# Two-layer graph network on one core: which count lets GpSimd issue the next gathers of the score stage

## The reference

```python
def _gatv2(x, edge_index, Wl, Wr, att, gat_bias):
    src, dst = (edge_index[0], edge_index[1])
    xl = (x @ Wl).reshape(-1, HEADS, C)
    xr = (x @ Wr).reshape(-1, HEADS, C)
    h = jax.nn.leaky_relu(xl[src] + xr[dst], NEG_SLOPE)
    e = jnp.einsum('ehc,hc->eh', h, att)
    m = jax.ops.segment_max(e, dst, num_segments=N_NODES)
    ex = jnp.exp(e - m[dst])
    denom = jax.ops.segment_sum(ex, dst, num_segments=N_NODES)
    alpha = ex / (denom[dst] + 1e-16)
    msg = alpha[..., None] * xl[src]
    out = jax.ops.segment_sum(msg, dst, num_segments=N_NODES)
...
h = jnp.maximum(_layernorm(x, axis=-1), 0.0)
x = x + _L0_gnn_ref(h, edge_index, ...)
h = jnp.maximum(_layernorm(x, axis=-1), 0.0)
x = x + _L1_gnn_ref(h, src, dst, L1_gnn_ln_g, L1_gnn_ln_b, L1_gnn_W, L1_gnn_b)
```

## Time and profile before

| | us |
|---|---|
| median of 3 runs | 1217.9 |
| the runs | 1214.75 to 1218.52 |
| span of the profiled execution | 1275.0 |
| VectorE busy | 1030.6 (81%) |
| TensorE busy | 1089.3 (85%) |
| ScalarE busy | 681.0 (53%) |
| GpSimd busy | 436.6 (34%) |
| L587, 352 gathers of both stages | 356.8 busy, 235.7 idle before them |
| L1569, 88 weightings | 107.7 busy, 54.4 idle before them |
| L1573, 88 sums | 107.3 busy, 2.7 idle before them |

### The profile page before, as it was taken

One profiled execution on the slowest core, in us unless ns is written; L12 is line 12 of the kernel. 1 busy time (PEld: TensorE's weight loads), 2 busy tenths in 40 slices (PEclk: granted clock), 3 DMA queues, 4 the chain that ended last, 5 costly groups with the idle time before them and its releaser, 6 DMA issues.

```text
span 1275.0 us, 16061 instructions
## 1 busy us (share of the span) xinstructions
PE 1089.3 (85%) x5027; PEld 793.4 (62%) x5047; DVE 1030.6 (81%) x1478; ACT 681.0 (53%) x1264; POOL 436.6 (34%) x412
## 2 busy tenths in 40 slices
PE   3979879566766666499999999799999999999998
PEld 2578456444544444245555555598888888889896
DVE  8999999778777887899999999876766869583934
ACT  4601300465565654478888888767555674232420
POOL 2072073565555666177766665000002100000000
PEclk9989989888777876599999999799999999999999
DMA  5000001566565658266667666400000211000002
GB/s 187 34 10 15 25 10 34 150 168 173 165 173 160 181 166 193 59 165 194 194 191 195 191 191 153 141 1 18 9 9 25 65 38 46 1 18 25 1 1 82
DMA packets 43436, 122.85 MB, mean 96 GB/s; under 512 B 7838, under 2 KB 8626, under 8 KB 43352
## 3 DMA queue, kind: packets, MB, share of 16 engines
q0 software_dynamic: 29184, 93.81, 27.5%
q1 hardware_dynamic: 14168, 27.98, 6.6%
HBM read 116.13 MB, written 5.59 MB: 95 GB/s over the span
## 4 chain that ended last, share of the span: by engine, by line
PE 46%; ACT 7%; DVE 2%; issue 1%; ACTq 1%; another core or an unknown queue 0%; DVEq 0%
PE bank L891 11%; PE bank L851 8%; PE bank L837 8%; PE bank L784 7%; PE bank L907 7%; PE bank L795 5%; ACT counts L1077 3%; ACT hot L964 2%; ACT arena L962 2%; PE bank L822 1%; ACTq L1073 0%; DVE stat L1269 0%; PE bank L625 0%; DVE w_lo L1637 0%
## 5 line engine op out<-in xcount | busy, mean ns | idle before, releaser
L587 POOL DMA_INDIRECT arena<-left_table,arena x352 | 356.8, 1013 | 235.7 <-issue 85.4
L784 PE MATMUL bank<-arena,hot 128*128 128x512 f32 x352 | 177.5, 620 | 0.9 <-DVE den_parts L1661 0.9
L718 PE MATMUL bank<-xr_hi,hot_t 128*128 x176 | 94.9, 539 | 97.3 <-ACT bank L1050 66.7
L1569 DVE SCALAR_TENSOR_TENSOR arena<-bank,arena 128x1024 f32<-128x1024 f32 x88 | 107.7, 1224 | 54.4 <-PE bank L718 29.9
L891 PE MATMUL bank<-counts_r,ns 128*128 128x512 f32 (+2 forms) x720 | 137.1, 349 | 0.0
L891 PEld LDWEIGHTS bank<-counts_r,ns 128*128 128x128 f32 x720 | 125.6, 188 | 10.4
L1077 ACT ACTIVATE counts<-bank 128x1280 f32 x88 | 108.9, 1238 | 37.6 <-issue 21.1
L795 PE MATMUL bank<-arena 128*128 128x512 bf16 (+1 forms) x508 | 110.0, 349 | 9.2 <-ACT counts L1077 5.6
L1050 ACT ACTIVATE bank<-arena 128x1024 f32<-128x1024 f32 x88 | 90.2, 1025 | 42.8 <-DMA arena<-left_table,arena 29.9
L718 PEld LDWEIGHTS bank<-xr_hi,hot_t 128*128 128x128 f32 x176 | 41.9, 238 | 110.4 <-issue 104.9
L1573 DVE TENSOR_REDUCE arena<-arena 128x16 f32<-128x1024 f32 x88 | 107.3, 1220 | 2.7
(11 more groups left out here) (258 smaller groups left out, 2256.2 us busy)
## 6 DMA issues: line engine op xcount, KB each, us to landing
arena<-left_table,arena POOLq DMA_INDIRECT x352
arena<-in_x_dram SPq DMA_DIRECT2D x18, 256.0 KB, 5.0
arena<-in_L_gnn_W_dram SPq DMA_DIRECT2D x8, 512.0 KB
arena<-in_L_gnn_W_dram SPq DMA_DIRECT2D x2, 1536.0 KB, 11.1
arena<-in_L_gnn_W_dram SPq DMA_DIRECT2D x3, 1024.0 KB, 5.3
left_table<-arena SPq DMA_DIRECT2D x10, 260.0 KB, 2.0
out_dram<-state SPq DMA_DIRECT2D x9, 256.0 KB
arena<-in_L_gnn_Wl_dram SPq DMA_DIRECT2D x1, 1024.0 KB, 9.0
```

The lines of the kernel that those rows point to most:

```text
L587: g.indirect_dma_start(out=gathered[n % DEPTH][:, i, :], out_offset=None, in_=left_table, in_offset=bass.IndirectOffsetOnAxis(ap=src_of[:, ...
L718: ins_ = t.matmul(bank[:, rows_at(n) + i, :], mine, part[:, bass.ds(at, 1), :].rearrange("p b n -> p (b n)"), start=False, stop=(part is x ...
L784: t.matmul(bank[:, psum, :], as_float(hot[c % 4]), w[:, i, :], start=(i == 0), stop=(i == 1))
L1569: v.scalar_tensor_tensor(y, bank[:, at:at + 2, :], 0.0, over(att_relu, 1, 2), ALU.max, ALU.mult).then_inc(*rows_weighted.up())
```

## The change

The gates of the score stage's gathers are counts of VectorE instead of TensorE's. The first gather of pair n waits for `rows_weighted` of pair n-4, the second for `pair_scored` of pair n-4. The first four pairs have no gate. The wait for the free buffer stays, and the gathers of the second stage have no gate, as before.

```diff
-    LEADS = 4, 3
+    LEAD = 4
...
-            def gather(n, rows=None):
+            def gather(n, scoring=False):
 
                 for i in range(2):
                     c = 2 * n + i
-                    if rows and n + 1 - rows[i] > 0:
-                        g.wait_ge(rows_added.sem, n + 1 - rows[i])
+                    if scoring and n >= LEAD:
+                        g.wait_ge((pair_scored if i else rows_weighted).sem, n - LEAD + 1)
                     g.indirect_dma_start(out=gathered[n % DEPTH][:, i, :], out_offset=None, in_=left_table,
...
             for n in range(NG):
                 if n >= DEPTH:
                     g.wait_ge(sources_kept.sem, n - DEPTH + 1)
-                gather(n, LEADS)
+                gather(n, True)
```

## The result

The changed kernel takes 1225.4 us (median of 4 runs, 1224.1 to 1227.1), the kernel before 1217.6 (median of 4, 1214.8 to 1218.5): a ratio of 1.0065 with an interval of 1.0048 to 1.0083. It is slower by 7.8 us, over twice the 0.3% that a measurement can tell from no change.

A forecast was written before the change was run, and what follows sets the result against it. VectorE was taken to bound the score stage at 2.51 us a pair. Adding 0 per pair, 0 for held places, 0 at the start and 1.1 at the end to 1217.9 gave 1219.0 us, range 1211 to 1226.

The forecast's parts named there:

- the lost margin: Slower rival, chance 0.26: gather data arrives too late for the reduced lead; 1229 us, or mildly 1222 to 1226.
- The gates and what stands behind them: GpSimd's queue in the score stage: only the awaited count differs, only gathers stand behind it, only the seed waits for those.
- The new loop: Score stage, VectorE taking pair n-4 to pair n ready: 8.8 us against 10.0 for four pairs; cost 0 per pair.
- GpSimd's start: Term of the loop: GpSimd starts a gather 0.3 us after what it waits for, like its gap between gathers.
- Issue to seed: Term of the loop: from the second gather's issue to ScalarE's seed, 3.45 us, read from pair 19.
- The rival's point: Slower rival's threshold: data over 4.6 us from its gather's issue now reaches VectorE; before the change it took 8.5.
- the rival's strong form: Slower rival at a usual data distance of 5.1 us: 22 loops each 0.5 us longer, 11 us, 1229 in all.
- The end: Last pairs of the score stage, holding padding: cost between 0 and 3.4 us, taken as 1.1.
- The held places: Score stage waits for TensorE's late reports: a second gather goes about 1.0 us earlier, booked as a gain of 0.
- No row decides it: Whether timed runs have TensorE's late reports: margin 1.2 us without, 3.0 with; the loop closes within VectorE's time either way.
- What would show it: Profile signs: L587 waits for L1569 and L1573, idle before L1569 50 to 58 us, stage 282 within 3.
- The rival *faster: Score stage gathers freed from TensorE's late reports remove some seed waits: 6 us gained, 1212 us, chance 0.22.

The follow-up runs named there:

- LEADS = 5, 4: The kernel before, with one pair more of lead on each of its gates by TensorE's count; ratio 0.9965 to the kernel before, without late TensorE reports.
- LEAD = 5: The changed kernel with both VectorE counts taken five pairs back, not four; 1.0070, 1.0076 and 1.0050 to the kernel before, on chips with late TensorE reports.
- LEAD = 3: The changed kernel with both VectorE counts taken three pairs back, not four; ratio 1.0173 to the kernel before, on a chip otherwise showing late TensorE reports.

## Why the prediction held in its range and not in its sum, step by step

The range of 1211 to 1226 held the time, 0.6 us from its end, and the direction came out as summed. The sum did not hold: it gave 1.1 us more than before, within what a measurement can't tell from nothing, and 7.8 were measured. It was the rival *the lost margin*, in its mild form (1222 to 1226), with a chance of 0.26. So the range is right through that rival and not through the mechanism that I held for the likeliest, and that is luck in part.

**The gates and what stands behind them**: as told. No instruction's duration changed, and only gathers wait there.

**The new loop of 8.8 us with 1.2 us of cover** is the step that failed. The direction was right, 4 us of margin went, but two terms of what was left were too small. Pair 24 in the profile of after, with VectorE's weighting of pair 20 at its start and that of pair 24 at its end:

```profile
280.94 1.22 DVE L1569 SCALAR_TENSOR_TENSOR arena<-bank,arena 128x1024 f32<-128x1024 f32 x1
...
282.91 0.94 POOL L587 DMA_INDIRECT arena<-left_table,arena  x1 [0.32 <-issue]
...
284.16 0.95 POOL L587 DMA_INDIRECT arena<-left_table,arena  x1 [0.30 <-issue]
...
287.74 1.03 ACT L1050 ACTIVATE bank<-arena 128x1024 f32<-128x1024 f32 x1 [0.99 <-DMA arena<-left_table,arena]
...
289.85 0.40 PE L718 MATMUL bank<-xr_lo,hot_t 128*128 x1
...
290.99 1.22 DVE L1569 SCALAR_TENSOR_TENSOR arena<-bank,arena 128x1024 f32<-128x1024 f32 x1
```

1.22 (weighting) + 0.75 (until the first gather starts) + 1.25 (until the second does) + 3.58 (until the seed) + 2.51 (until the rows are added, at 290.25) = 9.31 us, and VectorE takes four pairs in 10.05. Two terms were mis-sized:

- *GpSimd's start*, booked at 0.3 us behind the sums. The first gather starts 0.75 us behind the weighting (median over pairs 10 to 79, and the least as well), and the second 1.25 later: 1.22 + 0.75 + 1.25 = 3.22 where I had 2.47 + 0.3 = 2.77. With the same 0.75 behind the sums the second gate would give 2.47 + 0.75 = 3.22 as well, so the two gates ask for the same moment and the second adds nothing to the first. The term is 0.45 us too small.
- *Issue to seed*, booked at 3.45 us from a single pair, which lies near the quickest of all. In the profile of after it is 3.76 at the median of the 38 seeds of pairs 10 to 79 that wait for their data, and 5.04 at the worst. That is not a matter of the quiet chip: read in the same way, the profile of before itself gives 3.80 (20 seeds, 3.35 to 5.16), and the two other held ones 3.78 and 3.77. The term is 0.31 us too small, and the trace at hand would have shown it. The Trainium skill, DMA: Bandwidth & Descriptors, section "Latency and other measured facts", has the access to HBM grow with its load; these profiles don't show it in the calm part of the stage, where 3.80 goes with 166 GB/s and 3.76 with 197 (225 to 450 us of each).

In place of 8.8 the loop is 1.22 + 0.75 + 1.25 + 3.76 + 2.47 + 0.1 = 9.55, and the cover 0.5 us, not 1.2. The rows are ready 0.51 us (median) before VectorE takes them, where I expected 1 to 1.5; with LEADS = 5, 4 it is 3.7. Half a microsecond is eaten by anything. Pair 56 shows how, in the timeline of after:

```profile
369.61 0.95 POOL L587 DMA_INDIRECT arena<-left_table,arena  x1 [2.05 <-issue]
...
373.00 1.03 ACT L1050 ACTIVATE bank<-arena 128x1024 f32<-128x1024 f32 x1 [2.80 <-DMA arena<-left_table,arena]
...
375.66 1.23 DVE L1569 SCALAR_TENSOR_TENSOR arena<-bank,arena 128x1024 f32<-128x1024 f32 x1 [1.01 <-PE bank L718]
```

One gather that starts late for no reason that the profile shows, and VectorE loses 1.0 us that it never makes up. Before pair 83 L1569 waits 7.0 of its 11.7 us for L718. This place is 1.0 of them; from 378 to 400 us, where 2.8 more of them stand, the granted clock of TensorE is 0.73 of full speed, against 1.00 in the stretch of pair 24 (280 to 291 us). What each of the others comes of was not traced.

**The rival's point, data over 4.6 us away.** As the calm loop really runs, it is 3.76 + 0.5, about 4.3 us. My figure for the rival's strong form, a usual 5.1, didn't come; the usual distance stayed under the point, and only the spread went over it (4 of the 38 seeds). That is why it is the mild form.

**The end, booked at 1.1 us between 0 and 3.4.** The waits before the weightings of pairs 83 to 87 are 1.09, 0.73, 0.95, 0.80 and 1.15 us, 4.7 in all. How much of it the change added can't be read off, since the kernel before waits there too: 3.5, 3.4 and 3.8 us in its held profiles. With 83 pairs that hold edges and the first called 0, the padding begins with pair 83, not with 84 as I had it, so five such pairs wait and not four. Pair 87 in the timeline of after, from the weighting of pair 83 on:

```profile
450.67 1.23 DVE L1569 SCALAR_TENSOR_TENSOR arena<-bank,arena 128x1024 f32<-128x1024 f32 x1 [1.09 <-PE bank L718]
...
452.65 0.94 POOL L587 DMA_INDIRECT arena<-left_table,arena  x1 [1.38 <-DVE arena L1569]
...
453.90 0.95 POOL L587 DMA_INDIRECT arena<-left_table,arena  x1 [0.30 <-issue]
...
460.76 1.03 ACT L1050 ACTIVATE bank<-arena 128x1024 f32<-128x1024 f32 x1 [2.47 <-DMA arena<-left_table,arena]
...
463.48 0.63 PE L718 MATMUL bank<-xr_lo,hot_t 128*128 x1
464.21 1.23 DVE L1569 SCALAR_TENSOR_TENSOR arena<-bank,arena 128x1024 f32<-128x1024 f32 x1 [1.15 <-PE bank L718]
```

The loop closes to the hundredth: 1.23 + 0.75 + 1.25 + 6.86 + 3.35 + 0.10 = 13.54 us for four pairs, 3.39 each against 2.51. The prediction had 5.40 us for the data of such pairs; here the four seeds of 84 to 87 start 5.88 to 6.86 us behind their second gather, and with TensorE at the lower of its clocks (a granted clock of 0.50 from 452 to 464 us and 0.63 us a matmul, where pair 24 has 1.00 and 0.40) seed to rows takes 3.35, not 2.47. Against LEADS = 5, 4, where none of pairs 83 to 87 makes VectorE wait over 0.04 us, nearly the whole 4.7 us is a loss of the late gates. The choice within the bounds was thus the second error: I took the low side as "nearer to the one execution that I can see", and that one was held.

**The held places, booked at 0.** On quiet chips there are none, on held chips the change makes them longer (23.9 against 14 to 19 us of "remote" waits), and there too it ends 0.7% slower. The change does touch TensorE's late reports, although I had written that I know of no way: fewer waits of VectorE for them, 9 against 12 to 15, and longer ones.

**No row decides it.** True, and more than I made of it: the span of 57 us above the runs was the sign that profile and times are of different conditions. The gap lies in the same places: between the two profiles the score stage differs by 279.4 - 239.0 = 40.4 us, the weighted sum stage, where the same gathers run again, by 7.9, and all the rest together by 3.8.

**What would show it.** L587 waits for L1569 as said (57.3 us on a held chip), hardly ever for L1573 (0.3 us), since the second gather comes free of its first at the moment when the sums would let it go. The idle time and the stage's length came out far from 54.4 and 282, by the quiet chip far more than by the change.

**The rival *faster***: the gathers were freed from TensorE's counts, and it brought no gain. Its mechanism needs seeds that wait for data and carry VectorE with them; the later gates made more of those (49, where LEADS = 5, 4 has 6), not fewer.

What stays open: the kernel before has no profile on a quiet chip, so its own idle time there is not measured, only that its time lies between those of LEADS = 5, 4 and the change. A lead of 5 by VectorE's counts wasn't run on a quiet chip, so whether the loss is in the lead alone, or partly in the 0.75 us that a count of VectorE takes, isn't separated; by the sum, 2.51 us more lead would cover it. Why LEADS = 5, 4 gains 0.35% over before isn't explained by the prediction's sum, which gives before a margin of 5.1 us. That GpSimd's pauses let TensorE's reports through fits the order of events in the held profiles of before and only part of it in the others; no experiment shows it. And LEADS = 5, 4 wasn't run on a held chip: what it gains on a quiet one it might lose there, as LEAD = 5 and no gates did against before.

## What to carry to other kernels

Before moving a producer's gate, add up the whole loop by the path through the first of the issues behind it, with the wake-up and the slow half of the landings rather than one good one, and want more to spare than the spread of the landings: here a cover of 0.5 us, with seeds up to 1.3 us later than their median, goes with a loss of 0.65%, and one pair more of lead on the gates of before gained 0.35%. Hold the profile's span against the timed runs before anything else; when they are 5% apart, the waits that you see may not be in the times that you must predict, and each price near a threshold needs both cases. And try a new lead in both conditions: here each was tried in one alone, LEADS = 5, 4 on a quiet chip, where it gained, and LEAD = 5 on held ones, where it brought nothing.

## What the runs showed of the hardware

- GpSimd starts a waiting gather 0.75 us after the recorded end of VectorE's instruction, but 0.27 us after TensorE's (233.64 in the earlier trace rows, behind matmuls whose end is at 233.37). Ends of matmuls are modelled in the profile, so part of the difference may be in the record.
- The same kernel takes 1217 to 1218 us in some groups of runs and 1267 to 1276 in others, on one core. Between the two profiles of this case over nine tenths of the difference (48.3 of 52.1 us) lie in the two stages where GpSimd issues gathers while TensorE works. In the longer one TensorE's reports reach ScalarE, VectorE and GpSimd late. In the three held profiles of the kernel before all 41 waits of VectorE for them end 1.09 to 1.99 us after GpSimd's last gather; with more lead some end while GpSimd is busy with one.
- How many such waits VectorE has goes with the gates: 12 to 15 in the held profiles of before, 9 with the change, 11 to 16 with a lead of 5, 15 with no gates, none with LEAD = 3, where GpSimd pauses for over 0.4 us in 77 of the 88 pairs.
- The data of the padding pairs at the end of the stage took longer from issue to seed with the change, 5.2 to 6.9 us against 3.76 elsewhere, but 4.1 to 4.5 with LEAD = 3 on a held chip. So the padding alone doesn't set it.
